# Loading the next head's weights later and in three transfers on the SyncE queue of a gated-delta attention layer with a mixture of experts

## The chip, the cores and the metric

The kernel runs on 1 core of one Trainium2 chip (trn2). The metric is the device time of one execution in microseconds (us); lower is better. The time before is 2320.44 us, the median of 3 runs (2314.27 to 2321.96). "Round" below means one pass through the kernel's hand-written instruction lists; there are 64 of them, and the profile's times inside a round are in us from the start of the span.

## The reference

The input is a batch of 4 sequences of 512 tokens with 256 features. The layer is a gated delta-rule attention with 16 key heads and 2 value heads for each of them, and then a mixture of 8 experts with a shared one. Cut to what matters for this case:

```python
mixed = silu(causal_conv(x @ w_qkv, conv_w))
z = x @ w_z
q, k, v = split(mixed)
for t in range(S):
    state = state * exp(g_t)
    delta = (v_t - k_t @ state) * b_t
    state = state + outer(k_t, delta)
    out_t = q_t @ state
o = rmsnorm(out * silu(z)) * norm_gamma
x = layernorm(x + o @ w_out)
x = layernorm(x + moe(rmsnorm(x)) + shared_expert(rmsnorm(x)))
```

## The kernel before, in words

One **body** is one key head of one sequence: 16 heads times 4 sequences make 64 bodies, numbered n, with head n // 4. Each body cuts its 512 tokens into 4 chunks of 128 and has 8 cells of 128 by 128 (4 chunks, 2 value heads). A body projects its q, k, v and z from x and the head's weights (`proj`, `gate`), convolves them, forms the products of keys and queries, and inverts eight triangular matrices of 128 by 128. It then walks the four chunks (`read`, `solve`, `write`, `out`), gates and normalises, and adds its share of the output projection (`project`) into an accumulator in SBUF.

**The inverse** is grown in six levels. At each level TensorE does a `join` (L1099), VectorE masks it into `N` (L1369), TensorE does a `growx` (L1109), ScalarE copies the result into `X` (L1288), and SyncE issues a DMA transpose of `X` into `XT` (L878, called `flip`). The `growx` of level i + 1 reads the `XT` that flip i makes, so that the six levels are a ring through TensorE, VectorE, ScalarE and the DMA queue. `x0` (L884) is the transpose that starts the inverse of a body, and the `join` of level 0 reads it.

**The order** is written out by hand. The table `ORDER` has one list for each engine; an entry (name, i, ahead) in round k does the piece of body k + ahead. Every engine runs its list once a round, in order, and waits on semaphores. So the growx of levels 1 to 5 that run in round k belong to body k + 2.

**SyncE issues every DMA** of the kernel, all on one queue (q1). In a round it issues, in this order: the decay rows `ecb` (L863), flip 1, the four loads of `vT` (L860), the store `o_blocks` (L893), flip 2, the decay rows `egb` (L863), the four loads of `ogT` (L860), flip 3, flip 4, `x0`, flip 5, flip 0 and the store `v_blocks` (L887). An instruction of SyncE that waits holds up all that stand behind it.

**The weights of a head** are 768 KB in `w_kh` (two buffers, 128 partitions of 6 KB each: 256 columns of k and q, 256 of v, 256 of z, for two row tiles) and 256 KB of output weights in `wo_raw` (one buffer). The entry ("weights", 0, 4) stands second in SyncE's list. It acts in round k where k mod 4 is 1, and there loads head k // 4 + 2: it waits until TensorE has done the last projections with the buffer (`s_proj`, `s_zp`), issues the load of `w_kh` (L841), waits for `s_wog`, and issues the load of `wo_raw` (L844):

```python
sp.dma_start(w_kh[:, kh % 2], w_heads[kh].rearrange("p (t n) -> p t n", t=KT)).then_inc(s_w, 16)
if kh > 0:
    sp.wait_ge(s_wog, kh)
sp.dma_start(wo_raw[:, :, :], w_out[kh]).then_inc(s_wo, 16)
```

`s_wog` counts the times that GpSimd has scaled `wo_raw` by gamma into `wo` (`scale_wo`, L927); the new load overwrites what that reads. GpSimd does that scaling in the same round, in its third entry (`ogs` 1, behind `pow` and `ogs` 0: L1009, L1014, L1018), once ScalarE has summed the squares of the round's outputs. Loads in rounds 1, 5, ..., 53 make 14; those of heads 0 and 1 are issued before round 0. TensorE waits for `s_w` in the first projection of a head (L1047), which for head k // 4 + 2 comes four rounds later, at the start of round k + 4.

Of the kernel before, what the change touches and what calls it, by code (L numbers as in the profile page):

```python
# [12 lines left out]
B, SEQ, D = 4, 512, 256  # L13
CH = SEQ // P
KT = D // P
KH, VH = 16, 2
# [42 lines left out]
        ("mhi", 1, 3), ("pairs", 0, 3), ("mlo", 0, 3), ("keys", 0, 3), ("qe", 0, 2),  # L59
    ],  # L60
    "sync": [
        ("ecs", 0, 2), ("weights", 0, 4), ("flip", 1, 2), ("vld", 0, 2), ("ost", 0, 0), ("flip", 2, 2), ("egs", 0, 4),
        ("old", 0, 0), ("flip", 3, 2), ("flip", 4, 2), ("x0", 0, 3), ("flip", 5, 2), ("flip", 0, 3), ("vst", 0, 3),
    ],
}

# [1 line left out]
def rounds(order):  # L68

    most = max(ahead for _, _, ahead in order)  # L70
    for k in range(-most, BODIES):
        for name, i, ahead in order:
            if 0 <= k + ahead < BODIES:
                yield name, i, k + ahead


def build_kernel(nc, x_rows, x_cols, w_heads, w_ab, conv_w, dt_bias, a_log, gamma, w_out,
                 rms_w, router_w, gate_up, down, tri, levels16, neg_mask, ident16, iota8, exponents, out):
    ctx = ExitStack()
    with ctx:  # L80
        def sb(name, shape, dt=F32):
            return ctx.enter_context(nc.sbuf_tensor(name, shape, dt))

        def sem(name):
            return ctx.enter_context(nc.semaphore(name))
# [24 lines left out]
        w_kh = sb("w_kh", [P, 2, KT, 768])  # L110
        wo_raw = sb("wo_raw", [P, VH, D])
# [49 lines left out]
        s_w = sem("s_w")  # L161
        s_wo = sem("s_wo")
# [72 lines left out]
        s_wog = sem("s_wog")  # L235
# [29 lines left out]
        def flat(t):  # L265
            return t[:, :, :].rearrange("p a n -> p (a n)")
# [15 lines left out]
        def level(n, i):  # L282
            return 6 * (n // 2) + i + 1
# [200 lines left out]
        def moe_first(sp):  # L484
            sp.wait_ge(s_scan, 2 * BODIES)
            sp.dma_start(xg[0], x_rows[0:SEQ, :].rearrange("(c p) n -> p c n", p=P)).then_inc(s_xg, 16)

        def moe_weights(sp):
            sp.wait_ge(s_proj, 4 * BODIES)
            sp.wait_ge(s_silu, 4 * BODIES)  # L490
            sp.wait_ge(s_vst[(BODIES - 1) % 2], 16 * (BODIES // 2))
            sp.wait_ge(s_zp, 2 * BODIES)
            sp.dma_start(gu_routed, gate_up[:, 0:NE]).then_inc(s_mw, 16)
            sp.dma_start(dn_routed, down[:, 0:NE]).then_inc(s_mw, 16)
            sp.dma_start(gu_shared, gate_up[:, NE:NX]).then_inc(s_mw, 16)
            sp.dma_start(dn_shared, down[:, NE:NX]).then_inc(s_mw, 16)
# [325 lines left out]
        @block.sync  # L822
        def _(sp):
            def columns(b):
                sp.dma_start(xT[:, :, SEQ * b:SEQ * (b + 1)],
                             x_cols[:, SEQ * b:SEQ * (b + 1)].rearrange("(t p) n -> p t n", p=P)).then_inc(s_xin[b], 16)

            sp.dma_start(wab[:, :, :], w_ab.rearrange("(t p) n -> p t n", p=P)).then_inc(s_wab, 16)
            columns(0)
            sp.dma_start(vec32[:, 1, :], a_log).then_inc(s_early, 16)  # L830
            columns(1)
            sp.dma_start(vec32[:, 0, :], dt_bias).then_inc(s_early, 16)
            columns(2)
            sp.dma_start(tri_sb[:, :, :], tri).then_inc(s_early, 16)
            columns(3)

            def weights(kh):
                if kh > 1:
                    sp.wait_ge(s_proj, 4 * B * (kh - 1))
                    sp.wait_ge(s_zp, 2 * B * (kh - 1))  # L840
                sp.dma_start(w_kh[:, kh % 2], w_heads[kh].rearrange("p (t n) -> p t n", t=KT)).then_inc(s_w, 16)  # L841
                if kh > 0:
                    sp.wait_ge(s_wog, kh)
                sp.dma_start(wo_raw[:, :, :], w_out[kh]).then_inc(s_wo, 16)  # L844

            weights(0)
            for dst, src in (
                (cw_all[:, :, :], conv_w), (lev[:, :, :], levels16), (identh[:, :], ident16), (expo[:, :], exponents),
                (gam[:, :], gamma), (iota_sb[:, :], iota8), (rt_w[:, :, :], router_w), (rms_sb[:, :], rms_w),
            ):  # L850
                sp.dma_start(dst, src).then_inc(s_const, 16)
            for i in range(2):
                sp.wait_ge(s_row, i + 1)
                sp.dma_start(rows[i].rearrange("(j p) t -> p j t", p=P), row_t[i]).then_inc(s_rowd, 16)
            sp.wait_ge(s_rowd, 32)

            def load_blocks(dst, src, n, loaded):
                blocks_of = src[n % 2].rearrange("(a s) (b k) -> b s a k", a=Q32, b=Q32)
                for b in range(Q32):
                    sp.dma_start(dst[32 * b:32 * b + 32].rearrange("p a x r -> p a (x r)"), blocks_of[b]).then_inc(loaded[n % 2], 16)  # L860

            def decay_rows(dst, i, n, loaded):
                sp.dma_start(dst[:, n % 2], rows[i, CELLS * n:CELLS * (n + 1)].rearrange("x t -> (x t)")  # L863
                             .unsqueeze(0).broadcast_to([P, CELLS * P])).then_inc(loaded[n % 2], 16)

            def run(name, i, n):
                if name == "egs":
                    if n > 1:
                        sp.wait_ge(s_scan, 2 * (n - 1))
                    decay_rows(egb, 0, n, s_eg)  # L870
                elif name == "ecs":
                    if n > 1:
                        sp.wait_ge(s_qe, n - 1)
                    decay_rows(ecb, 1, n, s_ec)
                elif name == "flip":
                    p = n % 2
                    sp.wait_ge(s_x[p], level(n, i))
                    sp.dma_start_transpose(XT[:, p], X[:, p].rearrange("p a n -> p (a n)")).then_inc(s_xf[p], 16)  # L878
                elif name == "x0":
                    p = n % 2  # L880
                    sp.wait_ge(s_pair, 2 * n + 2)
                    if n > 1:
                        sp.wait_ge(s_resp, 2 * (n - 1))
                    sp.dma_start_transpose(X[:, p], XT[:, p].rearrange("p a n -> p (a n)")).then_inc(s_x0[p], 16)  # L884
                elif name == "vst":
                    sp.wait_ge(s_vt, n + 1)
                    sp.dma_start(v_blocks[n % 2], flat(conv[:, 2:4])).then_inc(s_vst[n % 2], 16)  # L887
                elif name == "vld":
                    sp.wait_ge(s_vst[n % 2], 16 * (n // 2 + 1))
                    load_blocks(vn, v_blocks, n, s_vld)  # L890
                elif name == "ost":
                    sp.wait_ge(s_ot, n + 1)
                    sp.dma_start(o_blocks[n % 2], flat(og2)).then_inc(s_ost[n % 2], 16)  # L893
                elif name == "old":
                    sp.wait_ge(s_ost[n % 2], 16 * (n // 2 + 1))
                    if n > 0:
                        sp.wait_ge(s_opp, 2 * n)
                    load_blocks(ogT4, o_blocks, n, s_old)
                elif name == "weights":
                    if n % B == 1 and n // B + 1 < KH:  # L900
                        weights(n // B + 1)

            for name, i, n in rounds(ORDER["sync"]):
                run(name, i, n)
                if (name, i, n) == ("flip", 0, BODIES - 1):
                    moe_first(sp)
                elif (name, i, n) == ("flip", 5, BODIES - 1):
                    moe_weights(sp)
            moe_rows(sp)
# [126 lines left out]
        def _(pe):  # L1036
            gates_tensor(pe)

            def run(name, i, n):
                p, q, head, b = n % 2, n % 3, n // B, n % B  # L1040
                w = w_kh[:, head % 2]
                later = n > 0
                if name == "proj":
                    j, k = divmod(i, KT)
                    g = COLS_OF[j]
                    if i == 0 and b == 0:
                        pe.wait_ge(s_w, 16 * (head + 1))  # L1047
                    if k == 0:
                        if j < 2 and later:
                            pe.wait_ge(s_zs, 2 * (n - 1) + j + 1)  # L1050
# [18 lines left out]
                elif name == "gate":  # L1069
# [3 lines left out]
                    t = b * CH + i  # L1073
# [141 lines left out]
            for name, i, n in rounds(ORDER["tensor"]):  # L1215
                run(name, i, n)
                if n == 0 and (name, i) == ("proj", 2):
                    decays_tensor(pe)
                drain(name, i, n)
# [295 lines left out]
```

## Time and profile before

| what | us |
|---|---|
| median of 3 runs | 2320.44 |
| lowest and highest run | 2314.27, 2321.96 |
| the profiled execution's own time | 2318.31 |
| its span | 2316.6 |
| TensorE busy (PE) | 2153.8, 93% |
| VectorE busy (DVE) | 1843.2, 80% |
| GpSimd busy (POOL) | 1224.3, 53% |
| ScalarE busy (ACT) | 1198.6, 52% |
| DMA queue q1, share of its 16 engines | 68.9% |

The profiled execution took 2318.31 us, of which its span is 2316.6 us and 1.7 us lie around it. PE is the matmul part of TensorE and PEld its weight loads; SPq is SyncE's queue of DMA issues. A row of a timeline gives start, duration, engine, line and operation, and in brackets how long the engine sat idle before it and what ended that. A DMA's row lasts as long as SyncE needs to issue it; the transfer lands later. PEclk is the TensorE clock that was granted, as a share of full speed.

### The profile page before, as it was taken

How to read it: one execution, taken by the hardware profiler on the slowest of the kernel's cores; microseconds unless marked ns; L12 is line 12 of the kernel's file. 1: busy time of each engine (PE TensorE's matmuls, PEld its weight loads, DVE VectorE, ACT ScalarE, POOL GpSimd, SP SyncE). 2: the span in 40 equal slices, each digit the busy share in tenths (PEclk: the TensorE clock that was granted, in tenths of full speed). 3: DMA queues.
4: the chain of work that ended last, by engine and by line, in shares of the span. 5: the costliest groups of instructions: out<-in, count | busy, mean ns of one | idle time of the engine just before them, and what ended most of it. 6: DMA issues, size and time to landing. Idle time of an engine off the chain costs nothing. (4 is left out here: it accounts for less than half of the span.)

```text
span 2316.6 us, 47612 instructions
## 1 busy us (share of the span) xinstructions
PE 2153.8 (93%) x16494; PEld 1561.7 (67%) x16494; DVE 1843.2 (80%) x3303; ACT 1198.6 (52%) x3805; POOL 1224.3 (53%) x1194
## 2 busy tenths in 40 slices
PE   6899999999999999999999999999999999977998
PEld 3667677666777676767777676767676776754665
DVE  4788788888888888888888887888888788853665
ACT  3555555555655555655555565555565555531110
POOL 3555566565666565566655565655566565530100
PEclk8999999999999999999999999999999999989999
DMA  4587777788777778777777777878878878761000
GB/s 138 130 174 165 181 157 165 158 167 183 165 164 167 162 169 183 171 169 162 166 163 169 183 166 163 161 164 172 183 164 161 157 155 172 156 166 37 28 10 19
DMA packets 597341, 349.81 MB, mean 151 GB/s; under 512 B 487664, under 2 KB 558704, under 8 KB 596848
## 3 DMA queue, kind: packets, MB, share of 16 engines
q1 hardware_dynamic: 597104, 346.78, 68.9%
q8 instruction: 133, 2.18, 0.4%
q14 instruction: 104, 0.85, 0.1%
HBM read 159.50 MB, written 69.73 MB: 99 GB/s over the span
## 5 line engine op out<-in xcount | busy, mean ns | idle before, releaser
L1343 DVE SCALAR_TENSOR_TENSOR conv<-bank,cw_all,conv 128x511 f32<-128x511 f32 (+2 forms) x768 | 568.1, 740 | 18.3 <-ACT conv L1235 6.9
L1056 PE MATMUL bank<-xT,w_kh 128*128 128x512 f32 x1024 | 559.6, 630 | 10.6 <-ACT kraw L1264 10.1
L1288 ACT ACTIVATE X<-bank 128x512 f16<-128x512 f32 x384 | 229.8, 598 | 286.0 <-PE bank L1109 285.9
L1369 DVE TENSOR_TENSOR N<-bank,lev 128x512 f16<-128x512 f32 x320 | 218.5, 683 | 151.1 <-PE bank L1099 151.0
L1235 ACT ACTIVATE conv<-bank,cw_all 128x512 f32<-128x512 f32 x256 | 175.9, 687 | 289.5 <-PE bank L1056 289.5
L1184 PE MATMUL bank<-ogT,wo 128*128 128x512 f32 x512 | 268.3, 628 | 24.4 <-DMA ogT<-o_blocks 23.9
L985 POOL TENSOR_SCALAR_AFFINE_SELECT mhiT<-m32T 128x512 f16<-128x512 f32 x128 | 131.2, 1025 | 255.6 <-DVE m32T L1355 255.6
L1075 PE MATMUL bank<-w_kh,xT 128*128 128x256 f32 x1024 | 248.9, 386 | 0.4 <-DVE conv L1343 0.4
L1075 PEld LDWEIGHTS bank<-w_kh,xT 128*128 128x128 f32 x1024 | 189.8, 192 | 54.0 <-DVE conv L1343 23.7
L1099 PEld LDWEIGHTS bank<-X,mhiT 128*128 128x128 f16 x3072 | 139.9, 98 | 122.4 <-issue 110.5
L1387 DVE SCALAR_TENSOR_TENSOR rhs<-bank,sc_all,vals 128x128 f32<-128x128 f32 x384 | 116.0, 344 | 108.2 <-PE bank L1136 108.2
L1293 ACT ACTIVATE U<-bank 128x256 f32<-128x256 f32 x256 | 99.9, 390 | 181.7 <-PE bank L1148 181.6
L963 POOL TENSOR_TENSOR decb<-tri_sb,bfac 128x1024 f32<-128x1024 f32 x64 | 121.4, 1896 | 126.1 <-DVE pT L1363 126.1
L1175 PE MATMUL bank<-U,pT 128*128 128x128 f32 x1024 | 187.4, 275 | 0.0
L1158 PEld LDWEIGHTS bank<-U,keys 128*128 128x128 f32 x768 | 121.1, 200 | 97.8 <-ACT U L1293 66.3
L1056 PEld LDWEIGHTS bank<-xT,w_kh 128*128 128x128 f32 x1024 | 163.2, 196 | 27.0 <-issue 18.7
L1258 ACT ACTIVATE sqj<-bank 128x128 f16<-128x128 f32 x512 | 134.4, 277 | 88.2 <-PE bank L1066 88.2
L1109 PE MATMUL bank<-N,XT 128*128 128x64 f16 x2560 | 127.7, 194 | 51.3 <-DMA XT<-X 49.1
L1109 PEld LDWEIGHTS bank<-N,XT 128*128 128x128 f16 x2560 | 108.3, 98 | 98.1 <-issue 84.0
L1099 PE MATMUL bank<-X,mhiT 128*128 128x64 f16 x3072 | 154.3, 193 | 8.6 <-DMA X<-XT 7.2
L1175 PEld LDWEIGHTS bank<-U,pT 128*128 128x128 f32 x1024 | 155.2, 192 | 3.7 <-issue 0.5
L1349 DVE TENSOR_TENSOR_SCAN decb<-egb,decb 128x512 f32<-128x512 f32 x128 | 155.5, 1215 | 0.0
(178 smaller groups left out, 4851.9 us busy)
## 6 DMA issues: line engine op xcount, KB each, us to landing
egb<-rows SPq DMA_DIRECT2D x64, 512.0 KB, 4.9
v_blocks<-conv SPq DMA_DIRECT2D x64, 512.0 KB, 3.4
ecb<-rows SPq DMA_DIRECT2D x64, 512.0 KB, 5.2
vT<-v_blocks SPq DMA_DIRECT2D x256, 128.0 KB, 3.2
o_blocks<-og SPq DMA_DIRECT2D x64, 512.0 KB, 3.7
ogT<-o_blocks SPq DMA_DIRECT2D x256, 128.0 KB, 4.3
w_kh<-w_heads SPq DMA_DIRECT2D x16, 768.0 KB, 7.4
XT<-X SPq DMA_TRANSPOSE x384, 3.6
```

The costliest lines, as they stand in the source:

```text
L1056: mm = pe.matmul(PB[j % 2][:, :], w[:, k, g * P:(g + 1) * P], xT[:, k, b * SEQ:(b + 1) * SEQ], start=(k == 0), stop=(k == KT - 1))
L1075: mm = pe.matmul(PB[h][:, 256 * c:256 * c + 256], xT[:, k, t * P:(t + 1) * P], w[:, k, 512:768], start=(k == 0), stop=(k == KT - 1))
L1099: mm = pe.matmul(IB[p][:, x * 64:(x + 1) * 64], mhiT[:, p, x, :], blocks(X[:, p, x:x + 1, :], i, 0), start=True, stop=True)
L1109: mm = pe.matmul(IB[p][:, x * 64:(x + 1) * 64], XT[:, p, x, :], (last_N[:, x, :] if i == 5 else N[:, p, x, :]), start=True, stop=True)
L1175: mm = pe.matmul(dst, pT[:, p, x, :], U[:, x, :], start=(c == 0), stop=True)
L1184: mm = pe.matmul(OB[h][:, :], wo[:, head % 2, v, h * P:(h + 1) * P], ogT4[:, :, v::VH].rearrange("p a c r -> p c a r"), start=(v == 0), st ...
L1235: act.activation(conv[:, g, :], PB[i % 2][:, :], ACT.Copy, scale=cw_all[:, head, g * TAPS + 3:g * TAPS + 4]).then_inc(s_tap, 1)
L1258: act.activation(sqj[:, i, c, :], PB[i][:, c * P:(c + 1) * P], ACT.Square, accum_out=ssum[:, p, i, c:c + 1]).then_inc(s_sq, 1)
L1288: act.activation(blocks(X[:, p], i, 0), packed(IB[p], i), ACT.Copy).then_inc(s_x[p], 1)
L1343: dve.scalar_tensor_tensor(conv[:, g, m:], PB[j % 2][:, 0:SEQ - m], cw_all[:, head, g * TAPS + 3 - m:g * TAPS + 4 - m], conv[:, g, m:], op ...
L1349: dve.tensor_tensor_scan(d, egb[:, p, 512 * i:512 * i + 512], d, 0.0, ALU.mult, ALU.add).then_inc(s_scan, 1)
L1369: dve.tensor_tensor(N[:, p].rearrange("p x (b s) -> p x b s", s=LEVELS[i]), packed(IB[p], i), blocks(lev[:, 1 + i:2 + i, :], i, 0).broadca ...
```

## The change

In SyncE's list the entry ("weights", 0, 4) moves from behind `ecs` to behind `flip` 3. It acts in three rounds out of four: in rounds with k mod 4 of 1, 2 and 3 it loads one third each of the head's `w_kh` (256 columns of both row tiles, 128 partitions of two pieces of 1 KB), and behind the third third, in the round with k mod 4 of 3, it waits for `s_wog` and loads `wo_raw`. TensorE waits for 48 steps of `s_w` a head where it waited for 16. Head 0 is loaded in three transfers before the constants.

```diff
     "sync": [
-        ("ecs", 0, 2), ("weights", 0, 4), ("flip", 1, 2), ("vld", 0, 2), ("ost", 0, 0), ("flip", 2, 2), ("egs", 0, 4),
-        ("old", 0, 0), ("flip", 3, 2), ("flip", 4, 2), ("x0", 0, 3), ("flip", 5, 2), ("flip", 0, 3), ("vst", 0, 3),
+        ("ecs", 0, 2), ("flip", 1, 2), ("vld", 0, 2), ("ost", 0, 0), ("flip", 2, 2), ("egs", 0, 4), ("old", 0, 0),
+        ("flip", 3, 2), ("weights", 0, 4), ("flip", 4, 2), ("x0", 0, 3), ("flip", 5, 2), ("flip", 0, 3),
+        ("vst", 0, 3),
     ],
...
-            def weights(kh):
-                if kh > 1:
+            def weights(kh, j):
+                third = slice(256 * j, 256 * (j + 1))
+                if j == 0 and kh > 1:
                     sp.wait_ge(s_proj, 4 * B * (kh - 1))
                     sp.wait_ge(s_zp, 2 * B * (kh - 1))
-                sp.dma_start(w_kh[:, kh % 2], w_heads[kh].rearrange("p (t n) -> p t n", t=KT)).then_inc(s_w, 16)
-                if kh > 0:
-                    sp.wait_ge(s_wog, kh)
-                sp.dma_start(wo_raw[:, :, :], w_out[kh]).then_inc(s_wo, 16)
-
-            weights(0)
+                sp.dma_start(w_kh[:, kh % 2, :, third],
+                             w_heads[kh].rearrange("p (t n) -> p t n", t=KT)[:, :, third]).then_inc(s_w, 16)
+                if j == 2:
+                    if kh > 0:
+                        sp.wait_ge(s_wog, kh)
+                    sp.dma_start(wo_raw[:, :, :], w_out[kh]).then_inc(s_wo, 16)
+
+            for j in range(3):
+                weights(0, j)
...
                 elif name == "weights":
-                    if n % B == 1 and n // B + 1 < KH:
-                        weights(n // B + 1)
+                    if n % B > 0 and n // B + 1 < KH:
+                        weights(n // B + 1, n % B - 1)
...
                     if i == 0 and b == 0:
-                        pe.wait_ge(s_w, 16 * (head + 1))
+                        pe.wait_ge(s_w, 48 * (head + 1))
```

The queue of SyncE in the kernel before, from the end of one round into the next, whose k mod 4 is 1 (`w_kh<-w_heads` is the load of the projection weights, `wo_raw<-w_out` that of the output weights; the `DMA_TRANSPOSE` behind them is flip 1):

```order
L887 DMA v_blocks<-conv 128x1024 [waits s_vt]
L863 DMA ecb<-rows 128x1024 [waits s_qe]
L841 DMA w_kh<-w_heads 128x1536 [waits s_zp,s_proj]
L844 DMA wo_raw<-w_out 128x512 [waits s_wog]
L878 DMA_TRANSPOSE XT<-X 128x8x128 [waits s_xq1]
L860 DMA vT<-v_blocks 32x4x256 [waits s_vst1]
L860 DMA vT<-v_blocks 32x4x256 x3
L893 DMA o_blocks<-og 128x1024 [waits s_ot]
L878 DMA_TRANSPOSE XT<-X 128x8x128 [waits s_xq1]
```

In the changed kernel flip 1 stands directly behind the `ecb` load in every round, and nothing that waits for `s_wog` stands ahead of it.

The queue of SyncE in the changed kernel, from flip 2 to `x0` of a round whose k mod 4 is 3 (lines have moved by 5; the second `DMA_TRANSPOSE XT<-X` is flip 3, the third flip 4, and `X<-XT` is `x0`):

```order
L883 DMA_TRANSPOSE XT<-X 128x8x128 [waits s_xq1]
L868 DMA egb<-rows 128x1024 [waits s_scan]
L865 DMA ogT<-o_blocks 32x4x256 [waits s_opp,s_ost1]
L865 DMA ogT<-o_blocks 32x4x256 x3
L883 DMA_TRANSPOSE XT<-X 128x8x128 [waits s_xq1]
L843 DMA w_kh<-w_heads 128x2x256
L848 DMA wo_raw<-w_out 128x512 [waits s_wog]
L883 DMA_TRANSPOSE XT<-X 128x8x128 [waits s_xq1]
L889 DMA_TRANSPOSE X<-XT 128x8x128 [waits s_resp,s_pair]
```

The rounds with k mod 4 of 1 and 2 have the `w_kh` row at the same place without the `wo_raw` row; in the kernel before flip 4 follows flip 3 directly in all rounds.

## Rows read from the trace of the kernel before

**Rows 1.** The page: busy time of each engine
```profile
PE 2153.8 (93%) x16494; PEld 1561.7 (67%) x16494; DVE 1843.2 (80%) x3303; ACT 1198.6 (52%) x3805; POOL 1224.3 (53%) x1194
```

**Rows 2.** Waits of SyncE's queue: us in total, times, longest us
```profile
SPq L844 <- POOL wo L927: 61.6, 14, 4.7
```

**Rows 3.** Timeline of SyncE, round 53 (a round with a load)
```profile
1790.41 0.33 SPq L844 DMA_DIRECT2D wo_raw<-w_out  x1
1790.79 1.24 SPq L878 DMA_TRANSPOSE XT<-X  x1
```

**Rows 4.** Chain that ended last, in order of time, in round 53
```profile
1789.38 1.01 POOL wo L927
...
1790.79 4.15 DMA XT<-X
```

**Rows 5.** Timeline of all engines, round 53: ScalarE's X, and TensorE's growx 2
```profile
1787.58 0.59 ACT L1288 ACTIVATE X<-bank 128x512 f16<-128x512 f32 x1
...
1795.07 0.39 PE L1109 MATMUL bank<-N,XT 128*128 128x64 f16 x8 [2.36 <-DMA XT<-X]
```

**Rows 6.** Windows, L1411 to L1411: 14 rounds with a load (behind (x): PEclk, DMA, GB/s)
```profile
1792.31:1826.74 34.43, 1.24 (x2) 0.95 0.82 164
sum 473.98, DVE 17.29; mean DVE 1.24
```

**Rows 7.** The same for the 42 rounds between; then round 57 (no load)
```profile
sum 1294.51, DVE 51.84; mean DVE 1.23
...
1921.16:1952.55 31.39, 1.24 (x2) 1.00 0.79 160
```

**Rows 8.** Windows, all engines: behind TensorE's wait of round 53 (PEclk third from the end)
```profile
1794.90:1798.50 3.60, 3.43 (x18) 2.42 (x19) 0.66 (x2) 1.50 (x3) 0.53 (x3) 0.59 1.37 272
```

**Rows 9.** Timeline of SyncE and TensorE, round 52 (no load): flip 4, growx 4 and 5, join 0
```profile
1774.73 1.23 SPq L878 DMA_TRANSPOSE XT<-X  x1
...
1773.67 0.40 PE L1109 MATMUL bank<-N,XT 128*128 128x64 f16 x8
1779.99 0.40 PE L1109 MATMUL bank<-last_N,XT 128*128 128x64 f16 x8
...
1780.22 0.40 PE L1099 MATMUL bank<-X,mhiT 128*128 128x64 f16 x8
```

**Rows 10.** One line's DMAs: flip 3 of round 52, its start and landing
```profile
L878 SPq DMA_TRANSPOSE XT<-X x1: 1237/1237/1237, 1768.0 to 1768.0; - x1
...
DMA to landing us min/median/max: 5.5/5.5/5.5
```

**Rows 11.** The same for flip 4 and then x0 of round 52
```profile
DMA to landing us min/median/max: 3.3/3.3/3.3
...
DMA to landing us min/median/max: 3.1/3.1/3.1
```

**Rows 12.** Windows: vT loads; w_kh load; behind flip 3 (last: PEclk, DMA share, GB/s)
```profile
1794.00:1796.00 2.00, 0.93 (x12) 0.96 (x13) 1.53 (x3) 0.50 (x1) 1.43 (x3) 0.88 1.15 217
...
1789.20:1791.60 2.40, 2.05 (x20) 1.71 (x19) 2.36 (x6) 1.22 (x3) 1.38 (x3) 1.00 0.90 366
1773.10:1775.40 2.30, 2.30 (x14) 1.07 (x13) 1.61 (x4) 1.29 (x4) 2.23 (x4) 1.00 0.00 0
```

**Rows 13.** One line's DMAs to landing: ecb in rounds 53 and 52; w_kh and wo_raw, all
```profile
DMA to landing us min/median/max: 5.4/5.4/5.4
...
DMA to landing us min/median/max: 4.5/4.5/4.5
...
DMA to landing us min/median/max: 5.7/7.4/8.9
...
DMA to landing us min/median/max: 2.8/3.3/8.7
```

**Rows 14.** Timeline of the start: head 0's weights issued; first projection
```profile
4.78 0.93 SPq L841 DMA_DIRECT2D w_kh<-w_heads  x1
...
16.46 2.84 PE L1056 MATMUL bank<-xT,w_kh 128*128 128x512 f32 x6
```

## The prediction

> **What bounds the kernel now.** I read the busy times first: TensorE is busy 93% of the span and nothing else is near it [rows 1]. That leaves little room, and the question is where its idle time sits. The waits of SyncE's queue answer it: the load of the output weights (L844) waited 14 times for GpSimd's scaling L927, 61.6 us in all, 4.4 us each [rows 2]. SyncE runs its list in order, so the reader should look at what stands behind that wait: flip 1. In round 53 GpSimd ends the scaling at 1790.40 (1789.38 + 1.01), the output weights are issued at 1790.41 and flip 1 at 1790.79 [rows 3, 4]. ScalarE had finished the X that this flip turns at 1788.17 (1787.58 + 0.59) [rows 5]. The flip is thus 2.6 us late, and lands 4.15 us after its issue. TensorE sat idle 2.36 us until it landed [rows 4, 5]. The chain of waits shows the same path: scaling, flip 1, growx 2.
>
> The windows from one round to the next give its price, since they hold everything that the stall drags along. The 14 rounds with a load take 473.98 us, 33.86 us each [rows 6]; the 42 between them take 1294.51 us, 30.82 us each [rows 7]. The difference is 3.04 us. It is not the scaling on GpSimd, nor the place in the group of four: round 57 scales weights too but loads none, and takes 31.39 us against 34.43 us for round 53 close by, again 3.04 us less [rows 6, 7]. Of these 3.04 us, 2.36 us are TensorE's wait. Behind it the granted clock falls: 0.59 on average over the next 3.6 us, where most of the time is spent at the lower level of 1.2 GHz [rows 8], and a round with a load has 0.95 where round 57 has 1.00 [rows 6, 7]. The rest of the 3.04 us is that.
>
> **The change part by part.**
>
> *Flip 1 comes free.* The load and the wait for s_wog no longer stand ahead of it, so in 14 rounds it is issued when its X is ready. TensorE does not wait, and so the clock does not fall. Gain: 14 x 3.04 = 42.5 us. The four vT loads and all later flips stand behind flip 1 and move up with it; they are in the 3.04 us.
>
> *SyncE's own time.* Each third costs one issue of up to 0.93 us and the output weights 0.33 us [rows 3, 14]. They stand between flip 3 and flip 4. In round 52 SyncE is free there from 1769.2 (1768.0 + 1.2) to 1774.73, 5.5 us [rows 9, 10], waiting for ScalarE's next X. Cost nothing; with that cover gone it would be 0.9 us in each of 42 rounds.
>
> *The transfers on the queue.* Flip 3 lands at 1773.5 (1768.0 + 5.5) [rows 10] and flip 4 is issued at 1774.73 [rows 9]; from 1773.10 to 1775.40 the queue moves nothing at all, 2.3 us [rows 12]. A third is 0.262 MB. At the 366 GB/s of the whole load's passage that is 0.7 us, at the 217 GB/s of the vT loads, whose pieces are small too, 1.2 us [rows 12]. I take the larger since the pieces are now 1 KB. It fits into 2.3 us. In the third round the output weights follow with 0.7 to 1.2 us: at most 2.4 us, still about the gap.
>
> *What is late next, if it does not fit.* Flip 4 lands at 1778.0 (1774.73 + 3.3) and growx 5 reads it at 1779.99, 2.0 us later; x0 is issued directly behind flip 4, at about 1776.1, lands at 1779.2, and join 0 starts at 1780.22, 1.0 us later [rows 9, 11]. So the transfers may hold the queue 2.3 + 1.0 = 3.3 us before anyone waits for x0. Cost nothing.
>
> *What stands just ahead of them.* This is the term without a row of its own. Flip 3 has no slack: it lands at 1773.5 and growx 4 starts at 1773.67 [rows 9, 10]. If a transfer that is issued behind it slows it, or the ogT loads ahead of it, each of 42 rounds pays. One bound is nothing; I see no gain in it. The other is the ecb load, which landed after 5.4 us in round 53 with the 768 KB directly behind it and after 4.5 us in round 52 without: 0.9 us [rows 13], 42 x 0.9 = 38 us. I take 0.1 us, 4 us in all: a third is a third of that load, and flips 4 and x0, which have no more than small pieces about them, land in 3.3 and 3.1 us although other transfers stand directly behind [rows 11], so a flip seems hardly to feel what follows it.
>
> *The waits that moved.* The third third comes in a round whose k mod 4 is 3; s_wog was raised two rounds earlier, so that wait is over when SyncE gets there. s_proj and s_zp were reached a round before the first third. TensorE needs the head at the start of the round after next, over one round (31 us) after the third third is issued, against a landing of 8.9 us at most for the whole load now [rows 13]. GpSimd's next scaling comes two rounds behind the new load of the output weights. All nothing.
>
> *The start.* Head 0 in three transfers costs SyncE two more issues, at most 1.9 us, ahead of the constants. Its load is issued at 4.78 and would have landed by 13.7 even with 8.9 us; the first projection runs at 16.46 [rows 13, 14], 2.8 us of slack. Nothing.
>
> Sum: 2318.3 - 42.5 + 4 = 2280 us, against the profiled execution, which lies 0.1% under the median of the runs shown.
>
> **A rule against the change.** By the Trainium skill, "DMA: Bandwidth & Descriptors", section "Anatomy of one DMA", each transfer costs about 2.0 us fixed plus its bytes at 436 GB/s, and by its section on measured bandwidth transfers should be gathered to 1 MiB or more. An estimate from that page: a third takes 2.6 us and output weights the same, 5.2 us behind flip 3 in each third round, 1.9 us over the 3.3 us above, 14 x 1.9 = 27 us given back, which would make the sum 2307 us. That page also says the fixed part is mostly latency until completion is reported, so the next transfer need not stand behind it; the rival below prices the case that it does.
>
> **The rivals.**
>
> *A. The forecast, 0.84.* 2272 to 2292 us.
>
> *B. The thirds slow what is just ahead of them, 0.08.* For it: the ecb load's 0.9 us, and flip 3's lack of slack. Against: the flips' own landings with transfers behind them. In full: 2318.3 - 42.5 + 38 = 2314 us, no change; at half strength 2295 us.
>
> *C. Landing times are paid in full on the queue, 0.03.* In the third round two transfers one behind the other, at 3.3 us each, the output weights' median landing [rows 13]: 6.6 - 3.3 = 3.3 us in 14 rounds, 46 us back, 2322 us, no change. Against it: 366 GB/s moved in the passage of the whole load [rows 12]. This is what the page's rule comes to, with the rows' durations.
>
> *D. Slower, 0.02.* Each third holds the queue so long that x0, and with it join 0, comes late in 42 rounds. It decides from 4.5 us a third, where 42 x (4.5 - 3.3) passes the 42.5 us gained and 7 us more. With 5.7 us, the quickest landing of a whole load [rows 13], it gives 42 x 2.4 = 101 us, 2377 us. Against it: the 2.3 us gap and the rates [rows 12].
>
> *E. The stall is only exchanged, 0.03.* Flip 1 is free but something else of the round, such as the store of the outputs, takes over half of it: 2318.3 - 21 = 2297 us. Against it: the 42 rounds and round 57.
>
> **How the numbers follow.** The predicted time is that of A. The range runs from 2272 us (the gain in full, no cost, and 4 us for the spread of the runs) to 2303 us (0.6 us for each third instead of 0.1, and E), and leaves out B in full, C and D. About 0.3%, 7 us, is what a measurement of this kernel can tell from no change. A, E and the weaker part of B are faster: 0.91. B in full and C are the same: 0.06. Slower: 0.03.
>
> **What would show it.** SyncE's wait for L927 gone from its list of waits; flip 1 issued within 0.1 us of its X in all rounds; TensorE's 2.36 us ahead of growx 2 gone; rounds with k mod 4 of 1 as long as the others, near 31 us, and the clock at 1.00 in them; flip 3's landing and the start of growx 4 as far from the round's L1411 as before, within 0.2 us. Wrong would be: 42 rounds longer by some tenths with flip 3 landing later (B), x0 landing less than 0.2 us ahead of join 0 (C, D), or a new wait of SyncE.

## The result and the profile after

The changed kernel takes 2288.3 us (median of 4 runs, 2286.49 to 2292.74) against 2319.1 us before (median of 4 runs, 2314.27 to 2321.96). The ratio is 0.9872 with a 95% interval of 0.9848 to 0.9896: 31 us or 1.3% faster. The forecast was 2280 us in a range of 2272 to 2303 us. Timed again in two later comparisons, on other runs of the kernel before, the change gave 0.9855 (0.9836 to 0.9875) and 0.9861 (0.9839 to 0.9883). The profiled execution took 2286.65 us.

The page of the changed kernel, its head and the busy times, to be held against [rows 1]:

```profile
span 2284.9 us, 47644 instructions
...
PE 2141.9 (94%) x16494; PEld 1553.1 (68%) x16494; DVE 1841.7 (81%) x3303; ACT 1198.3 (52%) x3805; POOL 1224.3 (54%) x1194
...
w_kh<-w_heads SPq DMA_DIRECT2D x48, 256.0 KB, 4.1
```

The span is 31.7 us shorter. TensorE is busy 11.9 us less with the same number of matmuls, which points to the clock; this comes back below. The 48 transfers are the thirds.

The waits of SyncE's queue in the changed kernel, against [rows 2] (us in total, times, longest us; a list of waits reads so everywhere below):

```profile
SPq L883 <- ACT X L1293: 756.4, 301, 6.1
SPq L898 <- DVE og L1416: 163.2, 64, 26.6
...
SPq L843 <- PE bank L1061: 7.2, 13, 0.6
```

No wait for GpSimd's scaling is left; 61.6 us in 14 waits were there before. The last row puts up to 0.6 us ahead of a first third down to a projection. The issues contradict it: in the timeline of round 53 below, the third goes out at 1773.52, 0.1 us after flip 3's issue ends (1772.18 + 1.24). It is no wait.

TensorE's waits for flips and for the loads of `ogT`, which `project` reads, before and then in the changed kernel:

```profile
PE bank L1109 <- DMA XT<-X: 49.1, 35, 3.6
PE bank L1184 <- DMA ogT<-o_blocks: 23.9, 22, 9.0
```

```profile
PE bank L1189 <- DMA ogT<-o_blocks: 34.7, 39, 9.0
PE bank L1114 <- DMA XT<-X: 18.9, 27, 1.8
```

The waits for flips fell by 30.2 us, but those for `ogT` grew by 10.8 us. Another wait took part of the time over; "Why the prediction was right" comes back to it.

SyncE's timeline in round 53, against [rows 3]; L883 is the flip: flip 1, then, with flip 2 left out, flip 3 and flip 4:

```profile
1760.58 1.24 SPq L883 DMA_TRANSPOSE XT<-X  x1
1761.86 2.00 SPq L865 DMA_DIRECT2D vT<-v_blocks  x4
...
1772.18 1.24 SPq L883 DMA_TRANSPOSE XT<-X  x1
1773.52 0.57 SPq L843 DMA_DIRECT2D w_kh<-w_heads  x1
1778.82 1.26 SPq L883 DMA_TRANSPOSE XT<-X  x1
```

The same round on ScalarE and TensorE, against [rows 5]:

```profile
1759.97 0.59 ACT L1293 ACTIVATE X<-bank 128x512 f16<-128x512 f32 x1
...
1764.94 0.40 PE L1114 MATMUL bank<-N,XT 128*128 128x64 f16 x8
```

ScalarE ends X at 1760.56 and flip 1 is issued at 1760.58; in the other 13 rounds with k mod 4 of 1 it also goes out within 0.03 us, where it was 2.5 to 2.8 us late before. The growx that reads it has no bracket any more: TensorE came from the matmul before it without a gap, where it had sat idle 2.36 us.

The windows of the changed kernel, cut at L1416 (the line that was L1411) exactly as before. First the sum of the 14 rounds whose k mod 4 is 1, against [rows 6], then that of the 42 others, against [rows 7]:

```profile
1764.70:1796.58 31.88, 1.24 (x1) 1.00 0.82 163
sum 436.55, DVE 17.29; mean DVE 1.23
...
sum 1300.77, DVE 51.86; mean DVE 1.23
```

The 14 rounds went from 33.86 to 31.18 us each, 37.4 us in all. The 42 others went from 30.82 to 30.97 us, 6.3 us the other way. Together that is 31.2 of the 31.7 us. The granted clock in round 53 is 1.00, where it was 0.95.

What goes on behind flip 3 is shown by three windows of round 53 (columns as in [rows 12]; the last three are the granted clock, the DMA share and GB/s):

```profile
1774.00:1776.40 2.40, 1.81 (x9) 1.25 (x7) 2.40 (x4) 0.69 (x1) 1.42 (x1) 1.00 1.23 67
1776.30:1777.60 1.30, 0.80 (x2) 0.30 (x2) 1.26 (x3) 0.00 (x0) 1.09 (x2) 1.00 1.02 282
1777.70:1779.20 1.50, 1.50 (x12) 0.95 (x12) 0.62 (x4) 1.00 (x3) 1.50 (x3) 1.00 0.00 0
```

The third passes at 282 GB/s within 1.3 us around the landing of flip 3 (issued at 1772.2, landed 5.4 us later), and then the queue still stands empty for 1.5 us before flip 4's data. The gap of 2.3 us was large enough, as the sum had it.

### The profile page after: what moved, and what is told of

Read it like the earlier page. It is cut to its first block, busy times and chain, and to the rows that moved or that the text cites. A ratio compares the mean times of both kernels' runs of the same rounds, so it can differ in the third digit from the quotient of the medians.

```text
span 2284.9 us, 47644 instructions
## 1 busy us (share of the span) xinstructions
PE 2141.9 (94%) x16494; PEld 1553.1 (68%) x16494; DVE 1841.7 (81%) x3303; ACT 1198.3 (52%) x3805; POOL 1224.3 (54%) x1194
## 4 chain that ended last, share of the span: by engine, by line
PE 59%; DMA 23%; DVE 7%; ACT 2%; SPq 2%; issue 2%; POOL 0%; POOLq 0%; DVEq 0%; ACTq 0%
PE bank L1061 11%; PE bank L1189 11%; DMA ogT<-o_blocks 10%; DMA XT<-X 7%; DMA o_blocks<-og 5%; PE bank L1080 5%; PE bank L566 5%; PE bank L1180 5%; PE bank L1179 4%; PE bank L1114 3%; PE bank L1153 3%; PE bank L582 2%; SPq L865 2%; PE bank L1141 2%; DVE og L1416 2%
## 5 line engine op out<-in xcount | busy, mean ns | idle before, releaser
L1061 PE MATMUL bank<-xT,w_kh 128*128 128x512 f32 x1024 | 549.0, 619 | 12.1 <-ACT kraw L1269 12.1
L1163 PEld LDWEIGHTS bank<-U,keys 128*128 128x128 f32 x768 | 116.2, 192 | 93.0 <-ACT U L1298 64.5
L1179 PE MATMUL bank<-S,qE 128*128 128x128 f32 x768 | 153.4, 281 | 0.0
```

Source lines behind the costliest of these rows:

```text
L1061: mm = pe.matmul(PB[j % 2][:, :], w[:, k, g * P:(g + 1) * P], xT[:, k, b * SEQ:(b + 1) * SEQ], start=(k == 0), stop=(k == KT - 1))
L1179: pe.matmul(dst, qE[:, p, x, :], S[:, c, v * P:(v + 1) * P], start=True, stop=False)
```

## The experiments

The kernels were timed in three sets, each with runs of the kernel before; a ratio is to the runs of its own set. The first set has a_again, e1, e2 and e3 (before: 2320.77 us), the second e6, e7, e4 and e5 (before: 2322.46 us), the third e8, e9 and a_third (before: 2321.59 us). The second has no run of the changed kernel, so its kernels are held by ratio against the change's 0.9855 to 0.9872. The theories are named in the expectations on record.

### The changed kernel once more (a_again)

> The changed kernel once more, as the standard of this call: 2286 to 2293 us. Theory S (the wait for the scaling ahead of flip 1 was the cost), theory Q (the 1 MB of transfers ahead of flip 1 on the queue was the cost) and theory T (the split into thirds is needed for the gain) say the same of it.

Measured: 2287.84 us (5 runs) against 2320.77 us (9 runs), ratio 0.9855 (0.9836 to 0.9875). Its windows give a sharper idea of what one profile can say: 440.59 us for the 14 rounds and 1294.78 us for the 42, where the first profile of the same kernel had 436.55 and 1300.77 us. Such sums move by 4 to 6 us from one execution to the next. One round of the 14 stands out, the only one of the 42 such rounds in the three profiles of the changed kernel with a lower clock. Its window, and TensorE's wait in it, here ahead of growx 3:

```profile
523.53:557.19 33.66, 1.23 (x2) 0.95 0.74 158
```

```profile
531.73 0.39 PE L1114 MATMUL bank<-N,XT 128*128 128x64 f16 x8 [1.96 <-DMA XT<-X]
```

Without it the other 13 take 31.30 us each.

### The load stays ahead of flip 1, only the wait moves (e1_load_stays)

Against the kernel before:

```diff
-        ("old", 0, 0), ("flip", 3, 2), ("flip", 4, 2), ("x0", 0, 3), ...
+        ("old", 0, 0), ("flip", 3, 2), ("wraw", 0, 4), ("flip", 4, 2), ("x0", 0, 3), ...
+                elif name == "wraw":
+                    if n % B == 1 and n // B + 1 < KH:
+                        raw(n // B + 1)
```

`raw` holds the wait for s_wog and the load of wo_raw, which `weights` no longer has.

> The kernel before; only the load of wo_raw with its wait for s_wog goes behind flip 3 of the same round. The 768 KB of w_kh stay ahead of flip 1. S: flip 1 is issued when its X is ready, the gain is nearly whole, 2278 to 2290 us. Q: flip 1's data stand behind 768 KB that need 2.1 us at 366 GB/s, so most of the stall stays, 2305 to 2317 us. My own sum lies between: flip 1 lands some 2 us late against about 1 us of slack, 14 x 1.1 us is kept, 2292 to 2296 us.

Measured: 2303.9 us (4 runs), ratio 0.9926 (0.9900 to 0.9952), half of the gain. Round 53: the load and flip 1 in SyncE's timeline, growx 2 in TensorE's, and the flip's landing in the view of one line:

```profile
1770.50 0.76 SPq L841 DMA_DIRECT2D w_kh<-w_heads  x1
1773.55 1.28 SPq L881 DMA_TRANSPOSE XT<-X  x1
```

```profile
1779.95 0.39 PE L1115 MATMUL bank<-N,XT 128*128 128x64 f16 x8 [1.88 <-DMA XT<-X]
```

```profile
DMA to landing us min/median/max: 6.3/6.3/6.3
```

The flip is issued in time and then lands only after 6.3 us, where in the changed kernel it lands after 3.1 us: its data stand behind the 768 KB. TensorE waits 1.88 us. So the queue of transfers alone makes a stall too, even though SyncE waits for nothing. Neither S nor Q is right by itself: 16 us of the stall are left (2303.9 against 2287.84 us in the same set), near the 14 x 1.1 us of my own sum. The time itself is above my 2292 to 2296 us, which started from the forecast's 2280 us, and just under Q's range.

### One transfer of 768 KB behind flip 3 (e2_one_piece)

Against the kernel before:

```diff
-        ("ecs", 0, 2), ("weights", 0, 4), ("flip", 1, 2), ...
-        ("old", 0, 0), ("flip", 3, 2), ("flip", 4, 2), ("x0", 0, 3), ...
+        ("ecs", 0, 2), ("flip", 1, 2), ...
+        ("old", 0, 0), ("flip", 3, 2), ("weights", 0, 4), ("flip", 4, 2), ("x0", 0, 3), ...
```

> The kernel before; the whole entry (768 KB and 256 KB, in one round out of four) goes behind flip 3. S: as fast as the changed kernel or a few us faster, since only 14 rounds have a transfer behind flip 3 where the changed kernel has 42: 2278 to 2290 us. T: 1 MB behind flip 3 holds the queue for about 2.8 us, past the 2.3 us gap, and x0 and flip 4 come late, 14 us or more slower than the changed kernel, 2302 us or above.

Measured: 2288.16 us (5 runs), ratio 0.9867 (0.9848 to 0.9886), the same as the change. Its windows, 14 rounds and then 42:

```profile
sum 438.52, DVE 17.25; mean DVE 1.23
...
sum 1295.85, DVE 51.81; mean DVE 1.23
```

T is wrong: at the new place the split into thirds is not needed. The 14 rounds take 31.32 us each with 1 MB behind flip 3.

### The wait alone ahead of flip 1 (e3_wait_alone)

Against the changed kernel:

```diff
-        ("ecs", 0, 2), ("flip", 1, 2), ...
+        ("ecs", 0, 2), ("wogwait", 0, 4), ("flip", 1, 2), ...
+                elif name == "wogwait":
+                    if n % B == 1 and 0 < n // B and n // B + 1 < KH:
+                        sp.wait_ge(s_wog, n // B + 1)
```

> The changed kernel, with the wait for s_wog put back at its old place ahead of flip 1, and no transfer with it. S: flip 1 is issued 2.2 us late again in 14 rounds; with about 1 us of slack that is 14 x 1.2 to 14 x 2.4 us (the upper end if the clock falls again): 2305 to 2321 us. Q: without transfers ahead of flip 1 the wait costs little, 2288 to 2293 us.

Measured: 2299.39 us (4 runs), ratio 0.9903 (0.9888 to 0.9918), 11.5 us over the changed kernel of the same set. In round 53 flip 1 is issued at 1767.52 and lands 3.1 us later, and TensorE waits 0.80 us. The last row below is the sum of the 14 windows:

```profile
1767.52 1.24 SPq L883 DMA_TRANSPOSE XT<-X  x1
```

```profile
1770.72 0.39 PE L1117 MATMUL bank<-N,XT 128*128 128x64 f16 x8 [0.80 <-DMA XT<-X]
```

```profile
sum 444.37, DVE 17.26; mean DVE 1.23
```

The 14 rounds take 31.74 us each in this profile, 4 to 8 us more in all than the 440.59 and 436.55 us of the changed kernel, and the clock stays at 1.00 in every one of them. The profiled execution is the fastest of the four (2291.51 us, the others 2299 us and more), so it shows less than the 11.5 us between the medians. The wait costs, but only about a third of the whole. The median is above Q's 2288 to 2293 us and below S's 2305 to 2321 us.

### No loads at all (e6_no_loads)

Against the changed kernel; it leaves out the loads of heads 2 to 15, and TensorE and GpSimd go on with the weights of heads 0 and 1:

```diff
-                    if n % B > 0 and n // B + 1 < KH:
+                    if n % B > 0 and n // B + 1 < 2:
-                pool.wait_ge(s_wo, 16 * (kh + 1))
+                pool.wait_ge(s_wo, 16 * min(kh + 1, 2))
-                        pe.wait_ge(s_w, 48 * (head + 1))
+                        pe.wait_ge(s_w, 48 * min(head + 1, 2))
```

> The changed kernel without the loads of heads 2 to 15 (no w_kh, no wo_raw; TensorE and GpSimd go on with what heads 0 and 1 left). It shows what a round takes with nothing behind flip 3. Theory B (each third costs by slowing flip 3 and the ogT loads ahead of it): some 6 us faster than the changed kernel, 2280 to 2283 us, with the rounds whose k mod 4 is 1 at 30.8 us. Theory N (the thirds cost nothing; the rounds with k mod 4 of 1 are longer by themselves, and I set their floor too low by the mean of the others): as fast as the changed kernel within 3 us, 2285 to 2291 us, and these rounds keep 31.2 us or more.

Measured: 2285.27 us (6 runs) against 2322.46 us (11 runs), ratio 0.9851 (0.9824 to 0.9878), not to be told from the change. Its windows, the 14 rounds and then the 42:

```profile
sum 437.90, DVE 17.27; mean DVE 1.23
...
sum 1298.45, DVE 51.83; mean DVE 1.23
```

With no transfer of weights in any of these rounds, the rounds with k mod 4 of 1 still take 31.28 us and the others 30.92 us. Theory N holds and B falls: the thirds cost nothing that these runs can show, and those 14 rounds are longer by 0.36 us for another reason. The interval is some 6 us to either side, so a cost of a few us in all would not be seen.

### No scaling on GpSimd (e7_no_scaling)

Against the changed kernel; it leaves out the scaling for heads 2 to 15:

```diff
-                    if i == 1 and n % B == 1 and n // B + 1 < KH:
+                    if i == 1 and n % B == 1 and n // B + 1 < 2:
                         scale_wo(n // B + 1)
-                        sp.wait_ge(s_wog, kh)
+                        sp.wait_ge(s_wog, min(kh, 2))
-                        pe.wait_ge(s_wog, head + 1)
+                        pe.wait_ge(s_wog, min(head + 1, 2))
```

> The changed kernel with all its loads, without GpSimd's scaling of the output weights for heads 2 to 15 (14 times 1.04 us in rounds with k mod 4 of 1). Theory G (the scaling delays what GpSimd does next, and that is why these rounds stay longer than the others): they fall to 30.8 us, 5 us faster than the changed kernel. Against it: GpSimd then waits 2.4 us for ScalarE's squares behind the scaling. Then no difference, 2285 to 2291 us.

Measured: 2289.36 us (6 runs), ratio 0.9864 (0.9838 to 0.9890): no difference to the change. The 14 rounds keep their length, 31.30 us:

```profile
sum 438.26, DVE 17.28; mean DVE 1.23
```

So the scaling is not the reason either.

### The transfers behind x0 (e4_behind_x0) and pieces of 2 KB (e5_2kb_pieces)

Against the changed kernel, e4 and then e5:

```diff
-        ("flip", 3, 2), ("weights", 0, 4), ("flip", 4, 2), ("x0", 0, 3), ("flip", 5, 2), ...
+        ("flip", 3, 2), ("flip", 4, 2), ("x0", 0, 3), ("weights", 0, 4), ("flip", 5, 2), ...
...
-                third = slice(256 * j, 256 * (j + 1))
+                third = slice(512 * j, 512 * (j + 1))
-                sp.dma_start(w_kh[:, kh % 2, :, third],
-                             w_heads[kh].rearrange("p (t n) -> p t n", t=KT)[:, :, third]).then_inc(s_w, 16)
+                sp.dma_start(w_kh[:, kh % 2].rearrange("p t n -> p (t n)")[:, third],
+                             w_heads[kh][:, third]).then_inc(s_w, 16)
```

> The changed kernel with the thirds and the output weights behind x0 instead of behind flip 3. Theory B: nothing without slack stands ahead of them there (x0 has 1.0 us), so it is 3 to 6 us faster, 2282 to 2285 us. Theory N: the same within 3 us, 2285 to 2291 us.

> The changed kernel with thirds of 512 neighbouring values of the 1536 in a partition, so pieces of 2 KB instead of two of 1 KB. If the size of the pieces costs anything (1.2 us against 0.7 us of queue for each third), it is hidden by the 2.3 us gap: 2285 to 2291 us, the same. If theory B holds and goes by the time on the queue, up to 3 us faster.

Measured: e4 2288.36 us (6 runs), ratio 0.9864 (0.9836 to 0.9891); e5 2287.3 us (4 runs), ratio 0.9851 (0.9816 to 0.9885). Both are the same as the change, as N says. Neither the neighbour ahead nor the size of the pieces matters here.

### Wait and output weights ahead of flip 1, the thirds behind flip 3 (e8_raw_ahead)

Against the changed kernel:

```diff
-        ("ecs", 0, 2), ("flip", 1, 2), ...
+        ("ecs", 0, 2), ("wraw", 0, 4), ("flip", 1, 2), ...
+                elif name == "wraw":
+                    if n % B == 1 and n // B + 1 < KH:
+                        raw(n // B + 1)
```

> The changed kernel with the output weights and their wait back at the old place ahead of flip 1 (round with k mod 4 of 1); the thirds of w_kh stay behind flip 3. Of the kernel before only the 768 KB ahead of flip 1 are missing. Theory O (these 768 KB passed while SyncE waited, so they cost nothing beside the wait; the wait and the 256 KB directly ahead of flip 1 make the whole stall): flip 1 lands 4.2 us after its issue, TensorE waits 2.5 us, the clock falls, 2312 to 2321 us. Theory P (each of the three parts has its own price, some 1 us a round): TensorE waits less, the clock seldom falls, 2300 to 2310 us.

Measured: 2313.17 us (12 runs) against 2321.59 us (17 runs), ratio 0.9961 (0.9944 to 0.9977), 23 us over the changed kernel of the same set (2290.1 us). The time falls into O's range at its low end, and the 768 KB are thus not quite free beside the wait: 8 us, 0.6 us a round. O's details did not come: the flip of round 53 landed 3.5 us after its issue and not 4.2, and TensorE waited 1.48 us there, 1.9 us on average over the 14 rounds, and not 2.5:

```profile
1783.15 0.34 SPq L849 DMA_DIRECT2D wo_raw<-w_out  x1
1783.54 1.24 SPq L885 DMA_TRANSPOSE XT<-X  x1
```

```profile
1787.22 0.39 PE L1119 MATMUL bank<-N,XT 128*128 128x64 f16 x8 [1.48 <-DMA XT<-X]
```

The windows show what decides the rest. Four of the 14 rounds (the number behind (x) is the granted clock), and the sum of the 14:

```profile
404.97:438.79 33.82, 1.24 (x1) 0.95 0.82 176
...
783.44:815.67 32.23, 1.23 (x1) 1.00 0.82 188
907.64:940.99 33.35, 1.24 (x1) 0.95 0.76 180
1033.18:1065.60 32.42, 1.24 (x2) 1.00 0.82 184
...
sum 458.91, DVE 17.29; mean DVE 1.23
```

Six of the 14 rounds have a clock of 0.95 and take 33.42 us on average, the eight with 1.00 take 32.30 us. The kernel before splits in the same way. Three of its 14 rounds kept 1.00:

```profile
534.27:566.87 32.60, 1.24 (x2) 1.00 0.84 178
...
910.40:943.44 33.04, 1.23 (x1) 1.00 0.82 171
1035.93:1068.96 33.03, 1.24 (x1) 1.00 0.89 174
```

They average 32.89 us, and the other eleven (473.98 - 98.67) / 11 = 34.12 us. So rounds with a fall are 1.1 to 1.2 us longer. Not all of that is the clock: they are also the rounds with the longer waits ahead of growx 2, on average 2.1 against 1.8 us in e8 and 2.6 against 2.3 us in the kernel before. With these 0.3 to 0.4 us taken off, the fall itself comes to some 0.8 us a round, an estimate, since no run changes the clock alone. That it stretches TensorE's work is to be seen in two such windows of the kernel before (the number behind the length is the busy time of TensorE, both times for 248 matmuls):

```profile
534.27:566.87 32.60, 29.42 (x248) 22.04 (x247) 26.68 (x47) 18.11 (x60) 18.55 (x18) 1.00 0.84 178
1412.37:1446.49 34.12, 31.16 (x248) 23.05 (x247) 26.70 (x46) 18.00 (x60) 18.55 (x18) 0.95 0.81 169
```

### The thirds ahead of flip 1, the wait behind flip 3 (e9_thirds_ahead)

Against the changed kernel:

```diff
-        ("ecs", 0, 2), ("flip", 1, 2), ...
-        ("flip", 3, 2), ("weights", 0, 4), ("flip", 4, 2), ...
+        ("ecs", 0, 2), ("weights", 0, 4), ("flip", 1, 2), ...
+        ("flip", 3, 2), ("wraw", 0, 4), ("flip", 4, 2), ...
+                elif name == "wraw":
+                    if n % B == 3 and n // B + 1 < KH:
+                        raw(n // B + 1)
```

> The changed kernel with the thirds of w_kh at the old place behind ecb and ahead of flip 1 (42 rounds), the output weights with their wait behind flip 3 as in the change. A third is on the queue for 0.7 to 1.2 us and flip 1 has about 1.0 us of slack. Theory K (only what goes past that slack costs): flip 1 lands about 1 us later, growx 2 about in time, 2286 to 2296 us. If every us ahead of flip 1 costs: 42 x 0.7 to 1.0 us, 2316 to 2330 us.

Measured: 2284.32 us (5 runs), ratio 0.9842 (0.9819 to 0.9864), at least as fast as the change. Flip 1 of round 53 lands 3.7 us after its issue instead of 3.1 us, and the waits of TensorE for flips are no longer than 1.6 us (us in total, times, longest us):

```profile
PE bank L1119 <- DMA XT<-X: 21.9, 31, 1.6
```

Theory K holds. 256 KB ahead of flip 1 fit into its slack, 768 KB (e1) did not. Here, at the old place, the split is worth about the 20 us between e1 and e9, which were timed in different sets (ratios 0.9926 and 0.9842) and also differ in the round in which the output weights go.

### The changed kernel a third time (a_third)

> The changed kernel again, as the standard of this call: 2286 to 2291 us.

Measured: 2290.1 us (5 runs) against 2321.59 us (17 runs), ratio 0.9861 (0.9839 to 0.9883).

## Why the prediction was right, and where its size was off

**The mechanism** was the one forecast: an in-order queue that waited for GpSimd with flip 1 behind it. SyncE's wait is gone, flip 1 goes out 0.02 us after its X, TensorE's 2.36 us are gone, and the clock is at 1.00 in all but one of those rounds (a_again has the one). Each of these was named ahead as what would show the step right. So was the distance of flip 3's landing and of growx 4 from the round's L1411: averaged over the 42 other rounds, both are 0.13 us later than before (12.17 against 12.04 us, 12.40 against 12.27 us), within the 0.2 us that were set, and e6, with no loads, has 12.10 and 12.35 us.

**The step that was mis-sized is the gain, "14 x 3.04 = 42.5 us".** It took the mean of the 42 other rounds, 30.82 us, as what a round with k mod 4 of 1 would take without the stall. It measured 31.18, 31.47 and 31.32 us in the three profiles of the changed kernel (436.55, 440.59 and 438.49 us for 14; the 31.47 holds the one round of 33.66 us), and 31.28 us with all loads left out (e6). From 33.86 us down to 31.28 us is 2.58 us, or 36 us for 14 rounds. The check with round 57 misled me. It held round 57's 31.39 us against round 53 alone, which at 34.43 us is 0.57 us above the mean of its kind, and that the difference was 3.04 us again was chance. Against the mean, 33.86 - 31.39 = 2.47 us would have given 34.6 us for 14 rounds and a sum of 2288 us. Even that would have been partly luck, for round 57 took 31.68, 31.27 and 31.94 us in the three profiles of the changed kernel, which does the same work there: one round is no floor to 0.3 us. The place in the group of four, which the prediction excluded by that one round, does matter: the loads left out, the rounds with k mod 4 of 1 are still the longest.

**What took the difference** is at least in part a wait that the stall had covered. In the 14 rounds TensorE waited for `ogT` ahead of `project` once, 1.1 us, in the kernel before; in the changed kernel these waits are 8.8, 9.0 and 7.9 us in its three profiles, and 7.9 us without loads (e6). The 42 other rounds had 12.0 us of them before, 4.0 us for 14 rounds, and only that much was in the mean that the prediction took as the floor. So 4 to 5 of the missing 6.4 us would be this wait, as far as a wait counts in full. Two neighbouring rounds of the changed kernel show how the length of a round goes with it. In round 53, 31.88 us long, TensorE waits 1.0 us for `ogT`; in round 54 it waits 0.2 us:

```profile
1796.58:1827.38 30.80, 1.24 (x1) 1.00 0.84 174
```

The landings of the four `ogT` loads in round 53, and then in round 54:

```profile
DMA to landing us min/median/max: 4.5/5.2/6.5
```

```profile
DMA to landing us min/median/max: 4.4/4.7/5.4
```

Flip 3, which stands behind these loads, lands 5.4 us after its issue in round 53 and 4.7 us in round 54. Why the loads land later in rounds with k mod 4 of 1 is open; it is not the weights' transfers (e6), nor the scaling (e7).

**The 4 us set down for what stands ahead of the thirds** were too much, if anything: with the transfers behind flip 3, behind x0, whole, in larger pieces, or not there at all, the times are 2285 to 2290 us. The ecb load's 0.9 us was a bad guide to a third of its size. The 6.3 us by which the 42 other rounds were longer in the first profile are within what such sums do: the same kernel had 1294.78 us in the second profile, 1300.66 us in the third, and the kernel without loads 1298.45 us. The two terms were off in opposite directions, the gain by 6.4 us and the cost by about 4 us, so that the forecast came nearer than its gain deserved: that part is luck.

**The range's upper end** of 2303 us is said to be 0.6 us for each third "and E". Each of the two alone gives about that (2301 us); both together would be 2322 us.

**Costs that were set at nothing** held: the two or three issues of SyncE in its 5 us of free time (0.57 us for a third), the waits that moved, the start. So did the 1.2 us for a third on the queue.

**The rivals.** B, the thirds slowing flip 3, is excluded by e6 and e4, in full and at half strength. C, landing times paid in full in the third rounds, is excluded by e2: there 768 KB and 256 KB follow one another behind flip 3 without a loss. With it falls, for this place, what the prediction drew from the Trainium skill, "DMA: Bandwidth & Descriptors" (about 2.0 us fixed for each transfer, in "Anatomy of one DMA", and the advice to gather them, in "Bandwidth"): 48 transfers of projection weights where 16 were cost nothing here, e2 against the change. Both sections give figures for transfers that GpSimd issues, which the prediction did not say; all of this kernel's are issued by SyncE. D did not occur. E did in small: the wait for `ogT` took over some 4 to 5 us, where E had it at half of the stall, 21 us.

**What the stall was made of**, by pieces that were put back one at a time: the wait alone 11.5 us (e3); the load alone 16 us (e1); wait and output weights 23 us (e8); all three 32 us. The pieces do not add up, and the time from X to flip 1's landing says why. Averaged over the 14 rounds it is 3.4 us in the changed kernel, 4.1 in e9, 5.5 in e3, 6.0 in e1, 6.3 in e8 and 7.0 in the kernel before. TensorE's wait ahead of growx 2 is, to 0.1 us, what goes past 4.4 us of it: nothing, nothing, 1.1, 1.6, 1.9 and 2.6 us. So the first microsecond is slack that each piece uses up for itself alone. And in the kernel before SyncE's wait and the load lie side by side, since the load passes partly while SyncE waits: 2.8 us of delay and a landing of 4.2 us, where the load alone made the landing 6.0 us. On the far side the fall of the clock adds to it: in the profiles, none of the 14 rounds shows it with the wait alone, two with the load alone, six in e8, eleven in the kernel before. Eleven times 0.8 us is 9 us, an estimate, somewhat under a third of what the change gained. In the prediction this was inside the 3.04 us without a size of its own.

## What to carry to other kernels

A wait on an in-order DMA queue is priced by what stands behind it, so a load that nobody needs for a long time should not be the one to wait ahead of a transfer on a tight ring; moving the entry by some places can be the whole change, and splitting it matters only where it still stands ahead of something with little slack. When the gain is a difference between rounds with and without the stall, take the floor from rounds of the same kind, by a kernel that leaves the suspected work out, and not from the mean of the others or from one round. Look for the wait that comes next, too: the stall may be hiding it (here the one for `ogT`). And look at the granted clock behind each wait of TensorE: where it fell here, behind waits of 1.9 to 3.6 us, a round lost some 0.8 us more, by the estimate under e8.

## What the runs showed that I had not expected

The fall of the granted clock came more often the longer TensorE's wait ahead of growx 2, with no length that parted the rounds. TensorE's waits for flips in the kernels e3, e1 and e8:

```profile
PE bank L1117 <- DMA XT<-X: 34.0, 39, 1.7
```

```profile
PE bank L1115 <- DMA XT<-X: 40.2, 37, 3.0
```

```profile
PE bank L1119 <- DMA XT<-X: 41.7, 35, 2.5
```

Averaged over the 14 rounds alone, the wait ahead of growx 2 is 1.1 us in e3, 1.6 us in e1, 1.9 us in e8 and 2.6 us in the kernel before, and the clock fell in none, two, six and eleven of them. Single rounds overlap. The clock fell behind the wait of 1.96 us in a_again, shown above, and in e1 it stayed at 1.00 in the round with this one:

```profile
1529.69 0.39 PE L1115 MATMUL bank<-N,XT 128*128 128x64 f16 x8 [2.45 <-DMA XT<-X]
```

Rounds of one kernel with the same order of work therefore differ by 1.1 to 1.2 us. And transfers that were a megabyte in all passed behind flip 3 in one go with no effect on the time that the runs show, on a queue that is busy for 70% of the span: what counted was the place on the queue, not the load on it.
